# Edge states of a graph layer: a one-pass spread of codes, another order at the experts' first products, 13 of 64 columns looked up

## The reference

```
h = (x_flat @ W_gat).reshape(M, HEADS, NUM_EXPERTS)
...
e = jax.nn.leaky_relu(a_src[src] + a_dst[dst], negative_slope=0.2)
e_max = jax.ops.segment_max(e, dst, num_segments=M)
ee = jnp.exp(e - e_max[dst])
denom = jax.ops.segment_sum(ee, dst, num_segments=M)
...
msg = h[src] * alpha[:, :, None]
agg = jax.ops.segment_sum(msg, dst, num_segments=M).reshape(M, HEADS * NUM_EXPERTS) + b_gat
...
for ei in range(NUM_EXPERTS):
    g = jnp.where(topk_i == ei, w, 0.0).sum(-1)
    hh = jax.nn.gelu(x @ W1[ei] + b1[ei], approximate=False)
    out = out + g[..., None] * (hh @ W2[ei] + b2[ei])
```

## Time and profile before

| | us |
|---|---|
| median of 3 timed runs (8279.27 to 8286.48) | 8283.25 |
| the profiled execution's own time | 8271.63 |
| its span, first to last instruction | 8269.9 |

### The profile page before, as it was taken

One profiled execution on the slowest core, in us unless ns is written; L12 is line 12 of the kernel. 1 busy time (PEld: TensorE's weight loads), 2 busy tenths in 40 slices (PEclk: granted clock), 3 DMA queues, 4 the chain that ended last, 5 costly groups with the idle time before them and its releaser, 6 DMA issues. The chain is left out here.

```text
span 8269.9 us, 97220 instructions
## 1 busy us (share of the span) xinstructions
PE 7135.9 (86%) x34853; PEld 5240.9 (63%) x34853; DVE 5283.9 (64%) x7812; ACT 2134.5 (26%) x4196; POOL 5025.1 (61%) x4822
## 2 busy tenths in 40 slices
PE   1888888599959999859999999999999999999668
PEld 0766666466633444347777777777777777777557
DVE  1765565467775543137777777777777776667678
ACT  0566555444422122111111111111111111111100
POOL 1333233477744636377777777777777777777473
PEclk6999999799979999979999999999999999999889
DMA  8111111021222534461111211111211111211257
GB/s 224 41 43 42 60 48 41 31 89 57 59 89 63 98 74 60 50 68 41 41 41 43 50 41 41 41 42 40 52 41 41 41 41 43 50 41 41 67 195 269
DMA packets 464347, 533.44 MB, mean 65 GB/s; under 512 B 243520, under 2 KB 386302, under 8 KB 441346
## 3 DMA queue, kind: packets, MB, share of 16 engines
q1 hardware_dynamic: 258082, 290.02, 13.1%
q0 software_dynamic: 149632, 72.60, 6.9%
q10 hardware_dynamic: 56416, 167.95, 5.8%
HBM read 263.12 MB, written 278.84 MB: 66 GB/s over the span
## 5 line engine op out<-in xcount | busy, mean ns | idle before, releaser
L1867 POOL DMA_INDIRECT e_row<-rows_dram,e_idx x3328 | 3163.1, 950 | 1022.0 <-issue 1013.0
L1762 PE MATMUL e_found<-e_pieces,e_hot 128*128 128x512 f32 x12288 | 3044.2, 400 | 0.0
L1762 PEld LDWEIGHTS e_found<-e_pieces,e_hot 128*128 128x128 f32 x12288 | 2245.8, 188 | 498.7
L1899 DVE TENSOR_TENSOR e_hot<-e_spread,e_lows 128x1024 fp32r<-128x1024 f32 x770 | 935.7, 1215 | 308.4 <-PE e_spread L1748 301.0
L1924 DVE TENSOR_TENSOR e_prod<-e_found,e_pick 128x512 f32<-128x512 f32 x768 | 530.3, 690 | 800.1 <-PE e_found L1762 794.7
L1832 ACT ACTIVATE e_ex<-e_dx 128x512 f32<-128x512 f32 x64 | 38.5, 601 | 2935.6 <-DVEq L1960 2935.6
L1929 DVE TENSOR_REDUCE e_row<-e_prod 128x16 f32<-128x512 f32 x768 | 785.5, 1023 | 0.0
L299 POOL COPY a_xr<-a_xp 128x1573 f32<-128x1573 f32 x104 | 204.8, 1974 | 862.1 <-DVE a_xp L591 561.8
L1775 PE MATMUL e_bank<-e_h,e_w 128*128 128x512 f32 x1024 | 526.5, 639 | 175.7 <-ACT e_hid L1822 175.7
L796 POOL DMA_INDIRECT yb_dram<-b_y,b_home x320 | 547.7, 1711 | 206.4 <-issue 103.3
L1784 PEld LDWEIGHTS e_bank<-e_w,e_hid 128*128 128x128 f32 x4096 | 501.6, 196 | 102.8 <-issue 102.8
(11 more groups left out here) (393 smaller groups left out, 9780.7 us busy)
## 6 DMA issues: line engine op xcount, KB each, us to landing
ys_dram<-e_y ACTq DMA_DIRECT2D x64, 1024.0 KB, 3.9
f_ye<-ys_dram SPq DMA_DIRECT2D x64, 1024.0 KB, 5.8
e_row<-rows_dram,e_idx POOLq DMA_INDIRECT x3328
res_dram<-e_st ACTq DMA_DIRECT2D x64, 768.0 KB, 5.5
xb_dram<-a_blanks ACTq DMA_DIRECT2D x8, 2580.0 KB
b_tok<-xb_dram SPq DMA_DIRECT2D x80, 258.0 KB, 2.7
a_xr<-in_x SPq DMA_DIRECT2D x8, 2048.0 KB, 8.3
a_xs<-in_x SPq DMA_DIRECT2D x8, 2048.0 KB, 8.1
```

Source lines behind the costliest of these rows:

```text
L1762: mm = nc.tensor.matmul(found[k % 2][:].rearrange("p s c -> p (s c)"), hot[:, k % 2, g], pieces[:, q, g].rearrange("p s c -> p (s c)"), st ...
L1867: nc.gpsimd.indirect_dma_start(row[:, s, u], None, rows, bass.IndirectOffsetOnAxis(ap=idx[:, s, u:u + 1], axis=0)).then_inc(gath[s], 16)
L1899: nc.vector.tensor_tensor(hot[:, k % 2], spread[:].unsqueeze(1).broadcast_to([P, HG, P]), lows[:].unsqueeze(2).broadcast_to([P, HG, P]), A ...
```

## The change

Twelve looked-up columns become 13, so 51 are gathered. The codes become float32r, and the identity that they are multiplied with is copied once into a float32r tile `unit`. In TensorE's order the second look-up of a chunk moves behind the first up.

```diff
--- before.py
+++ after.py
@@ -1640,7 +1640,7 @@
 def edge_states(nc, passed, rows, srcs, cont, v, res, hn, ys, ident, att_src, w, nodes, adst):
 
 
-    U, XG = 64, 12
+    U, XG = 64, 13
     UP = U - XG
     TURNS = FE // (2 * U)
     CHUNKS = 2 * TURNS
@@ -1653,7 +1653,8 @@
         allidx = sb("allidx", [P, FE + 2 * U], I32)
         idx = sb("idx", [P, 2, UP], I32)
         codei = sb("codei", [P, 2, CHUNKS + 1, XG], I32)
-        code = sb("code", [P, 2, XG])
+        code = sb("code", [P, 2, XG], mybir.dt.float32r)
+        unit = sb("unit", [P, P], mybir.dt.float32r)
         high = sb("high", [P, XG])
         lowi, lows = sb("lowi", [P, HG], I32), sb("lows", [P, HG])
         highi, highs = sb("highi", [P, HS], I32), sb("highs", [P, HS])
@@ -1745,7 +1746,7 @@
 
             def spread_code(k):
                 s, j = divmod(k % (2 * XG), XG)
-                nc.tensor.matmul(spread[:], code[:, s, j:j + 1].broadcast_to([P, P]), ident[:], start=True,
+                nc.tensor.matmul(spread[:], code[:, s, j:j + 1].broadcast_to([P, P]), unit[:], start=True,
                                  stop=True).then_inc(code_spread, 1)
 
             pe.wait_ge(consts, 64)
@@ -1786,9 +1787,9 @@
                     mm.then_inc(down_psum, 1)
 
                 for s in range(2):
-                    for j in range(2):
-                        look_up(XG * s + j)
+                    look_up(XG * s)
                     up(STEP * s)
+                    look_up(XG * s + 1)
                     for n in range(STEP * s, STEP * (s + 1)):
                         if n + 1 < STEP * (s + 1):
                             up(n + 1)
@@ -1890,6 +1891,7 @@
             nc.vector.tensor_copy(lows[:], lowi[:])
             nc.vector.tensor_copy(highs[:], highi[:])
             dve.wait_ge(init, 2)
+            nc.vector.tensor_copy(unit[:], ident[:])
             nc.vector.tensor_copy(code[:, 0], codei[:, 0, 0]).then_inc(coded, 1)
             dve.wait_ge(coded, 1)
             dve.wait_ge(consts, 64)
```

## The result

The changed kernel takes 8511.76 us (median of 4 runs, 8510.94 to 8518.6) against 8281.26: a ratio of 1.028 (95% interval 1.0262 to 1.0297). It is 230 us slower. The forecast was 8467, in a range of 8393 to 8541. The profiled execution took 8511.48 us, its span is 8509.8.

The account below looks back on a forecast made before the run. TensorE was taken to set the pace, with one wait a chunk fixed by VectorE and ScalarE. +2.81 us at full clock and +0.07 of clock, +2.88 x 64 = +184 us on the median 8283.25, gave 8467 us, range 8393 to 8541.

Parts of the forecast that it names:

- What bounds the kernel: Edge stage: TensorE sets 52.10 us of an undisturbed chunk, a path over VectorE and ScalarE the other 12.52.
- The move at nothing: TensorE's second look-up behind the first up: still ahead of the wait at the second up, so costed at nothing.
- The terms at full clock: Per undisturbed chunk: look-ups outside the wait +2.75 us, VectorE's path +0.06, together +2.81, from 64.62 to 67.43.
- the path: From a chunk's last look-up through VectorE and ScalarE to the second up: 12.52 us, growing by 0.06.
- The spread's price: TensorE's float32r spread in each look-up: one pass at 0.11 us instead of 0.22, bounded by nothing and 0.22.
- the row of 24 columns: Profile row of eleven TensorE passes, 0.112 us each, from which one spread pass was taken at 0.11.
- The clock: TensorE's lower clock after the wait at the second up: loss in proportion to the wait, 0.69 to 0.76, +0.07 us.
- the lower clock in every chunk: Rival: the longer wait costs each chunk 2.28 us of TensorE's clock, +4.40 a chunk, 8565 us; chance 0.04.

Follow-up runs that it names:

- e1: The kernel before with the float32r spread alone (12 columns, old order): 8243.6 us, 0.9965 of the kernel before.
- e3: The kernel before with 13 looked-up columns alone: 8565.43 us, 1.0355 of the kernel before.
- e6: e5 with 12 looked-up columns instead of 13: 8222.37 us, 0.9933 of the kernel before.
- e5: The changed kernel with ScalarE's two Gelus of a chunk's first expert ahead of the exponentials of the chunk before: 8183.22 us, 0.9889 of the kernel before.
- e2: The kernel before with the second look-up moved behind the first up alone: 8288.93 us, 1.0015 of the kernel before.
- e8: The kernel before with three added products, results overwritten, between first and second up: 8230.19 us, 0.995 of the kernel before.
- e4: The changed kernel with three added products, results overwritten, between second look-up and second up: 8389.28 us, 1.0141 of the kernel before.
- e9: The changed kernel with one added product instead of three in the wait at the second up: 8457.11 us, 1.0227 of the kernel before.
- e7: e5 with both look-ups ahead of the first up again, 13 columns: 8293.32 us, 1.0024 of the kernel before.

## Why the prediction was right, and which term was off

*What bounds the kernel.* Right: TensorE, with a wait that VectorE and ScalarE fix. e1 and e3 show that GpSimd set no pace before, e6 what it looks like when it does, and e5 that the wait was ScalarE's order.

*The move at nothing.* Right for the mechanism; e2 measured +0.15% (0.06 to 0.25), with the wait unchanged.

*The terms at full clock.* e8 and e4 are the two kernels without the clock's loss: 64.61 and 67.14 us a chunk, +2.53; forecast was +2.81. A look-up costs 3.83 instead of 3.85 (eleven of them, -0.22), and the path grew by 0.01 us in the mean of 63 borders (12.56 to 12.57) where 0.06 was forecast. The spread's price came out near the row of 24 columns: 0.13 us of its 0.22 saved. The Trainium skill ("TensorE: Matmul & The Clock Gate", "Back-to-back issue gap") states about 81 ns for a product of 128 columns in a stream with weight loads. The trace agrees: 0.09 us here (0.22 - 0.13).

*The clock.* This is the term that was mis-sized. The prediction scaled the loss with the length of the wait, 2.88 to 3.16, for +0.07 us a chunk. It went from 0.70 (65.31 - 64.61) to 1.85 (68.99 - 67.14), +1.15 a chunk or 74 us. The wait's length is not the measure: e3 has the waits of before (171.3 us against 175.7), and its 69.92 us a chunk (4404.78 / 63) against 64.61 + 4.02 = 68.63 is a loss of about 1.3; and e9 loses in one chunk and not in the next. What grew is the number of chunks that lose, from 23 of 63 to 62. The rival "the lower clock in every chunk" got 0.04; its mechanism came true, at a mean of 1.85 instead of 2.28 us. Together: 2.53 + 1.15 = 3.68 us a chunk, what the windows show. The forecast was 45 us short, and the measured time lies inside the range by luck: the bounds were those of the spread's price, and no bound was put on a dearer clock.

What stays open is what fixes, chunk for chunk, whether a wait costs clock. The runs show that it varies at the same wait, and how often it does, not by which rule.

## What to carry to other kernels

Moving work across a wait helps only if it crosses the waiting instruction, or if the engine that releases it can use the earlier input; here both look-ups and the first up stood ahead of the wait before and after. Cutting an instruction that TensorE does while a fixed path runs beside it only lengthens the wait (2.75 to 2.99 us in e1), and work shifted from an engine nobody waits for onto the one that sets the pace costs its full price. Reorder the releasing engine first (e5), then decide again how much work each engine gets.

## What the runs showed of the hardware

Three added products a chunk, 2.6 us in all, whose results nobody uses, made the kernel before 39 us faster, and the changed kernel 1.0141 instead of 1.028 times the kernel before, by keeping the granted clock at 1.00 behind the wait (e8, e4). A wait of some 3 us cost the changed kernel a mean of 1.85 us a chunk more than its own length, and one of 2.75 cost the kernel before 0.70: 62 and 23 of 63 chunks had a lower clock. A wait of 1.3 us cost none in 63 chunks (e7). And a float32r product of 128 columns added about 0.09 us to the stream, less than half of the 0.22 of a float32 one.
